# A perceiver layer with routed experts: matches, chunk constants and the first weight loads in other places of the last two tiles

## The reference

```python
x = x + xattn(layernorm(x), ctx, ...)      # 16 heads, each batch attends to its own 257 context rows of 192
x = x + local_attn(layernorm(x), ...)      # each row attends to rows i-2 .. i+2 of its batch
x = x + ffn(layernorm(x), ...)             # 8 experts, each token uses one: argmax(x @ Wr + br)
# ffn of expert e: gelu(x @ W1[e] + b1[e]) -> gelu(. @ W2[e] + b2[e]) -> . @ W3[e] + b3[e]
# sizes 256 -> 1024 -> 512 -> 256
```

## Time and profile before

| | |
|---|---|
| median of three runs | 708.14 us |
| the profiled execution | 709.04 us |
| its span, first to last instruction | 707.2 us |
| mean granted clock of TensorE | 0.992 |
| last scores of the tiles (batch 63) | start at 400.12 us |
| first row of experts enters TensorE | 428.59 us |
| busy: VectorE, ScalarE, GpSimd | 67%, 64%, 63% |

### The profile page before, as it was taken

The page is one execution under the profiler, slowest core; times in us unless marked ns, Lnnn a source line. Parts: engine busy times, 40 slices in busy tenths (PEclk is TensorE's granted clock), DMA queues, the critical chain, the costliest instruction groups (busy, mean ns, idle before and its releaser), DMA issues.

```text
span 707.2 us, 26666 instructions
## 1 busy us (share of the span) xinstructions
PE 687.9 (97%) x9301; PEld 581.3 (82%) x9302; DVE 475.2 (67%) x1462; ACT 451.4 (64%) x1073; POOL 442.9 (63%) x595
## 2 busy tenths in 40 slices
PE   8999999999999999999999969999999999999996
PEld 7888888888888888888888857888888888888885
DVE  4467777777777777777788889999943990278000
ACT  4656666666666676666666653666675757575753
POOL 6476665656566565656565635676767786777643
PEclk9999999999999999999999989999999999999998
DMA  7433233333323333343357324248034431262000
GB/s 214 119 87 85 70 78 96 93 82 82 96 72 93 94 88 74 76 96 91 87 154 246 129 83 165 97 123 300 23 106 159 170 113 60 82 223 65 25 7 1
DMA packets 56178, 74.35 MB, mean 105 GB/s; under 512 B 6589, under 2 KB 41950, under 8 KB 56128
## 3 DMA queue, kind: packets, MB, share of 16 engines
q1 hardware_dynamic: 49792, 60.63, 30.4%
q0 software_dynamic: 2992, 8.26, 3.8%
q10 hardware_dynamic: 3344, 4.80, 1.9%
HBM read 67.30 MB, written 7.27 MB: 105 GB/s over the span
## 4 chain that ended last, share of the span: by engine, by line
PE 92%; DVE 2%; issue 1%; ACT 1%; DMA 1%; POOL 1%; ACTq 0%; POOLq 0%; SPq 0%; DVEq 0%
PE ps_s L2023 18%; PE ps_kv L1603 12%; PE ps_kv L1611 11%; PE ps_p L1689 8%; PE ps_o L1675 6%; PE ps_s L1622 6%; PE ps_p L1971 4%; PE ps_kv L1971 4%; PE ps_o L2037 4%; PE ps_s L2002 2%; PE ps_m L1808 2%; PE ps_m L1754 2%; PE ps_m L1727 2%; PE ps_m L1812 2%; PE ps_s L2031 1%
## 5 line engine op out<-in xcount | busy, mean ns | idle before, releaser
L868 ACT ACTIVATE prob<-prob,neg_max 128x257 f32<-128x257 f32 x256 | 111.2, 501 | 42.9 <-DVE neg_max L1105 41.2
L1105 DVE CUSTOM_DVE_ANT_0 prob<-ps_s,mask_add 128x257 f32<-128x257 f32 x256 | 94.7, 421 | 64.0 <-PE ps_s L1622 63.7
L1573 DVE CAST w<-w_raw 128x512 fp32r<-128x512 f32 x94 | 71.0, 756 | 56.3 <-DMA w_raw<-in_L_ffn_W_dram 56.3
L1576 DVE TENSOR_TENSOR w<-w_raw,w 128x512 fp32r<-128x512 f32 x112 | 101.6, 910 | 3.7
L681 POOL TENSOR_TENSOR ctx_parts<-ctx_raw,ctx_parts 128x512 fp32r<-128x512 f32 x64 | 83.1, 1299 | 23.5 <-ACT ctx_parts L863 21.6
L2023 PE MATMUL ps_s<-w,h_hi 128*128 x368 | 91.1, 399 | 0.7 <-ACT h_hi L1017 0.6
L1611 PE MATMUL ps_kv<-wkv_hi,ctx_parts 128*128 128x256 f32 x512 | 84.6, 293 | 0.1
L1603 PE MATMUL ps_kv<-ctx_parts,wkv_hi 128*128 128x256 f32 x512 | 84.2, 292 | 0.2 <-POOL ctx_parts L681 0.2
L694 POOL COPY last_prob<-prob 128x4 f32<-128x4 f32 x64 | 12.1, 189 | 113.1 <-ACT prob L868 109.0
L876 ACT COPY v<-ps_kv 128x512 f32<-128x512 f32 x64 | 37.5, 587 | 70.2 <-PE ps_kv L1611 70.2
L806 POOL TENSOR_TENSOR h_lo<-h,h_hi 128x512 fp32r<-128x512 f32 x46 | 66.8, 1453 | 24.7 <-ACT h_hi L1004 19.8
(11 more groups left out here) (303 smaller groups left out, 1515.5 us busy)
## 6 DMA issues: line engine op xcount, KB each, us to landing
w_raw<-in_L_ffn_W_dram SPq DMA_DIRECT2D x24, 1024.0 KB, 7.1
ctx_raw<-in_ctx_turned_dram SPq DMA_DIRECT2D x63, 256.0 KB, 3.4
mask_add<-mask_dram SPq DMA_DIRECT2D x64, 128.5 KB, 3.3
w_raw<-in_L_ffn_W_dram SPq DMA_DIRECT2D x8, 512.0 KB, 3.6
rows_dram<-x3n ACTq DMA_DIRECT2D x15, 256.0 KB, 4.2
xt<-in_x_dram SPq DMA_DIRECT2D x16, 128.0 KB, 2.1
xr<-in_x_dram SPq DMA_DIRECT2D x16, 128.0 KB, 2.2
slot_x<-rows_dram,slot_ids POOLq DMA_INDIRECT x23, 3.9
```

The lines of the kernel that those rows point to most:

```text
L868: a.activation(prob[:, g, :], prob[:, g, :], ACT.Exp, bias=neg_max[:, g:g + 1], scale=-1.0).then_inc(exp_done, 1)
L1105: d.tensor_tensor_reduce(prob[:, r, :], ps_s[r][:, 0:J], mask_add[:, k, :], -(HD ** -0.5), 3.0e38, ALU.add, ALU.min, neg_max[:, r:r + 1]). ...
L1573: d.tensor_copy(w[:, b, HI, part], raw[:, b, part]).then_inc(rounded, 1)
L1576: last = d.tensor_tensor(w[:, b, LO, part], raw[:, b, part], f32(w[:, b, HI, part]), ALU.subtract)
```

## The change

Four edits.

1. Matches. VectorE takes eleven tiles and GpSimd five (tile 6 goes over). VectorE's matches of tiles 0 and 1 stand in (tile 15, k = 0) behind `number_many` and so ahead of the masks of that batch, that of tile 2 in (15, 1) ahead of the masks, those of tiles 3 and 4 at the two places in (15, 2). The match in (15, 3) and the one behind `number_single(1)` in `last_tile` are gone; the two later ones take tiles 5 and 6. GpSimd has no match in (15, 2); behind the tiles it makes four in a row (tiles 7 to 10), then the two scales, then the fifth (tile 11). TensorE's `fill_chunks` follow.
2. `place_chunks` goes from (1, 3) to (14, 3), behind `choose_single(0)` and ahead of the masks.
3. The eight `EARLY` loads are issued one after the other behind the load of the last residual rows (`xr` of tile 15), instead of one behind each mask load of tile 15, and one each behind four later events.
4. GpSimd issues the indirect load into `slot_x` (L780) ahead of `scale_of(2, 15)` and not behind it.

```diff
-        BY_DVE, BY_POOL = (0, 1, 2, 3, 12, 13, 4, 5, 14, 15), (6, 7, 8, 9, 10, 11)
+        BY_DVE, BY_POOL = (0, 1, 2, 3, 4, 12, 13, 5, 6, 14, 15), (7, 8, 9, 10, 11)
@@ SyncE
                     load_mask(T, b)
-                    if isinstance(T, int) and T == TILES - 1:
-                        load_part(*EARLY[b])
...
-            sp.wait_ge(m_emptied, turn(TILES - 2, 3) + 1)
-            load_x(xr, TILES - 2, xr_in)
-            load_part(*EARLY[BT])
-            sp.wait_ge(m_emptied, turn(TILES - 1, 3) + 1)
-            load_x(xr, TILES - 1, xr_in)
-            load_part(*EARLY[BT + 1])
-            sp.wait_ge(s_masked, GROUPS * B)
-            load_part(*EARLY[BT + 2])
-            sp.wait_ge(o_done, B)
-            load_part(*EARLY[BT + 3])
+            for T in (TILES - 2, TILES - 1):
+                sp.wait_ge(m_emptied, turn(T, 3) + 1)
+                load_x(xr, T, xr_in)
...
+            for part, e in EARLY:
+                load_part(part, e)
@@ GpSimd
-                    if isinstance(T, int) and (T, k) == (TILES - 1, 2):
-                        for t in BY_POOL[0:3]:
-                            match(t)
...
-            for t in BY_POOL[3:6]:
+            for t in BY_POOL[0:4]:
                 match(t)
             scale_of(1, TILES - 1)
             scale_of(2, TILES - 2)
+            match(BY_POOL[4])
...
-            scale_of(2, TILES - 1)
             g.indirect_dma_start(out=slot_x[:, AHEAD - 1, 0:D], ...)
+            scale_of(2, TILES - 1)
@@ VectorE
-                    if isinstance(T, int) and (T, k) == (1, 3):
-                        dve.wait_ge(router_consts, CONSTS)
-                        place_chunks()
...
                         choose_single(0)
+                        place_chunks()
                     if isinstance(T, int) and (T, k) == (TILES - 1, 0):
                         number_many()
+                        match(0)
+                        match(1)
+                    if isinstance(T, int) and (T, k) == (TILES - 1, 1):
+                        match(2)
                     if isinstance(T, int) and (T, k) == (TILES - 1, 2):
-                        match(0)
+                        match(3)
                     if isinstance(T, int) and (T, k) == (TILES - 1, 3):
                         number_single(0)
                         dve.wait_ge(logits_done, MANY + 2)
                         choose_single(1)
-                        match(2)
...
-                        match(1)
+                        match(4)
...
                 number_single(1)
-                match(3)
...
-                match(4)
+                match(5)
...
-                match(5)
+                match(6)
@@ TensorE
-                fill_chunks(0, 1, 2, 3, 6, 7, 8, 9)
+                fill_chunks(0, 1, 2, 3, 4, 7, 8, 9)
...
-                fill_chunks(10, 12, 11)
+                fill_chunks(10, 12)
...
-                fill_chunks(13, 4)
+                fill_chunks(13, 5)
...
-                fill_chunks(5)
+                fill_chunks(6, 11)
```

More of the change, by code:

```diff
@@ L535, in _ @@
             sp.dma_start(lbias[:, 4:6], lbv.rearrange("(c p) -> p c", p=P), allow_slow_non_contiguous=True).then_inc(router_in, 16)
[L537 to L547, removed]
             def ahead(T):
@@ L577, in _, with load_part @@
             ahead(TILES - 1)
-            sp.wait_ge(m_emptied, turn(TILES - 2, 3) + 1)
-            load_x(xr, TILES - 2, xr_in)
-            load_part(*EARLY[BT])
-            sp.wait_ge(m_emptied, turn(TILES - 1, 3) + 1)
-            load_x(xr, TILES - 1, xr_in)
-            load_part(*EARLY[BT + 1])
-            sp.wait_ge(s_masked, GROUPS * B)
-            load_part(*EARLY[BT + 2])
-            sp.wait_ge(o_done, B)
-            load_part(*EARLY[BT + 3])
+            for T in (TILES - 2, TILES - 1):
+                sp.wait_ge(m_emptied, turn(T, 3) + 1)
+                load_x(xr, T, xr_in)
+            def load_part(part, e):
+                _, raw, arrived, buffers, _ = PARTS[part]
+                b = turn_of(part, e) % buffers
+                if part == FIRST:
+                    w, n = W1[e], F1
+                elif part == THIRD:
+                    w, n = W3[e], D
+                else:
+                    half = HALVES.index(part)
+                    w, n = W2[e][half * F1 // 2:(half + 1) * F1 // 2, :], F2
+                sp.dma_start(raw[:, b, :].rearrange("p (k n) -> p k n", n=n), w.rearrange("(k p) n -> p k n", p=P)).then_inc(arrived[b], 16)
+            for part, e in EARLY:
+                load_part(part, e)
             sp.wait_ge(route, ROUTED)
@@ L705, in scale_of @@
                     g.tensor_tensor(spread[:, :], var_eps[i][:, :], rstd[i][:, :], ALU.mult).then_inc(spread_done, 1)
[L707 to L710, removed]
             def iteration(T):
@@ L767, in _, with match @@
             over_tiles(pool, iteration)
-            for t in BY_POOL[3:6]:
+            def match(t):
+                pool.wait_ge(many_step, 12)
+                g.tensor_scalar(of_chunk[:, t, :], chunk_number[:, :], chunk_at[:, t:t + 1], None, ALU.is_equal)
+                g.tensor_scalar(in_row[:, t, :], row_number[:, :], in_chunk[:, t:t + 1], tokens[:, t:t + 1], ALU.is_equal, ALU.mult).then_inc(matched_by_pool, 1)
+            for t in BY_POOL[0:4]:
                 match(t)
```

## The result

The changed kernel takes 713.1 us (711.92 to 714.16, six runs) against 708.69 us for the kernel before beside it (707.56 to 709.14): 1.0067 times as long, 95% interval 1.0056 to 1.0079. That is 4.4 us more; +1.5 was forecast, and the result lies above the range. The profiled execution took 714.08 us, its span is 712.3 us, and its mean granted clock 0.991; it is in the upper third of the 23 executions on record (711.92 to 714.81).

A forecast was written before the change was run, and what follows sets the result against it. TensorE was taken as the bound, except at batch 60, where VectorE's masks are. Terms +1.5 + 0.1 - 0.1 and zeros gave +1.5 us, 709.6 on the median of 708.14; eight-in-ten range 708.1 to 711.5.

The forecast's parts named there:

- The fall of the clock: Rival: between keys and values of batch 61 TensorE's longer gap halves the clock, +1.7 on top, 711.3 us; chance 0.18.
- Matches in (15, 0): Ahead of batch 60's masks: two matches, the first held up by GpSimd's shift, paid in full, +1.5 us.
- the rival without a hold-up: Rival at batch 60: GpSimd's shift does not hold `of_chunk`, the two matches cost 0.8, 708.9 us; chance 0.13.
- Match in (15, 1): Ahead of batch 61's masks: held up by GpSimd's shift, masks 0.7 late but mostly hidden, +0.1 us.
- the -0.1 of the sum: At (15, 3), one match less ahead of the masks of batch 63: -0.1 us, ends 0 and -0.5.
- `place_chunks` in (14, 3): Ahead of batch 59's masks: they start about 0.8 later, hidden by VectorE's idle time; cost 0, or 0.2 without cover.
- Where it leaves: In tile 1, where `place_chunks` is removed: the chain is TensorE's without a gap, gain 0.
- The loads: Eight loads behind `xr` of tile 15: hidden from ScalarE by 3 to 5 us of cover, 0, ends 0 and +0.5.
- the sign that I had named: The prediction is wrong if last scores to first expert row (28.5 us) changes by more than 0.3.
- Last tile's exchange of matches and the indirect load: In the last tile: VectorE's match gone, 0.1 gain, GpSimd's fourth match +0.1, indirect load in idle time 0; together 0.

The follow-up runs named there:

- only_matches_early: The kernel before, with the expert's number read by `value_load`, plus edits 1 and 4 (matches, indirect load) alone; 711.65 us, 1.0048 times the kernel before.
- the base: The kernel before with one edit, TensorE's slot loop reading the slot's expert by `value_load` into a plain register; 708.65 us, 1.0004 times the kernel before.
- loads_as_before: The changed kernel with the expert's number read by `value_load` and edit 3 undone, so loads spread as before; 713.16 us, 1.0070 times the kernel before.
- half pad: The kernel before, with `value_load`, `place_chunks` moved to tile 14 and two memsets put in (1, 3); 708.61 us, 1.0008 times the kernel before.

## Why the prediction was wrong

Two terms that stood in the sum with 0 failed: that `place_chunks` leaves its place ahead of the loop, which slowed the loop (+1.7 alone), and the burst of loads, which stopped TensorE (+0.8 alone). The fall of the clock stood outside the sum. What I had worked out from the rows, the hold-up in (15, 0), came as forecast.

**Matches in (15, 0): right in place, mechanism and size.** Forecast +1.5. From scores to masks it is 1.34 us more in the change and 1.46 in `only_matches_early`; `of_chunk` took 1.02, held by the shift, which is against the rival without a hold-up. Moved out of the shift's way they cost 0.2.

**Match in (15, 1): right, small.** Forecast +0.1, measured +0.15 to 0.2 from batch 60 to 63, held up by the shift until 392.1. The masks of batch 61 are 0.54 late (0.7 was forecast) and mostly covered. In (15, 3) the masks of batch 63 come 0.1 sooner after their scores, the -0.1 of the sum.

**`place_chunks` in (14, 3): right.** It hides: the masks of batch 59 come 0.76 later (0.8 was forecast), the scores of batch 60 only 0.13 later behind those of 59. **Where it leaves: wrong.** "In tile 1, where it leaves, the chain is TensorE's without a gap: gain 0." The 0 in the sum was the first failed step. I had bounded the edit by its own 0.8 us. What was removed is not only work but instructions ahead of a loop, and the loop ran 0.13 us a tile slower: +2.0 in the trace, +1.7 alone. The trace of before held a warning: that mask starts 1.08 us after the scores and the masks of the other batches 0.98, so at the jump VectorE and not TensorE was already the later one by 0.1.

**The loads: wrong.** "I take 0; ends 0 and +0.5." This is the second failed step. I asked who waits for the weights and for the rows beside them, and answered rightly that nobody does, though both came slower than I had counted: the first four loads landed 14.5 us after their first issue and not 9, and the store of rows at 400.73 took 6.9 us where 2.0 is usual. I did not ask what else uses those DMA engines. The instruction fetches do. In the trace 2.7 us of holes and the slower clock behind them make most of the +3.3 of the last tile, and the sign that I had named came: from the last scores to the first row it is 31.7 us and not 28.5. Alone the median is only +0.8; low executions are 1.9 to 2.7 above the base, the others 0.2 to 0.8. Both traces with the two holes are of low executions, so how large the holes are in the others is not shown.

**The clock: a rival that came beside the forecast.** I gave it 0.18 as something apart, at batch 61. It does happen there, in the trace of `loads_as_before`, and costs 1.2 us, not 1.7; the low executions of `only_matches_early` are 1.1 longer than the others, and where in them the clock fell no trace shows. In the profiled execution of the change it came at the second hole instead. Its weight should have been tied to the hold-up: the two kernels with the matches ahead of the masks and the early weights as before were low in seven of ten executions, against four of 97 of the kernel before.

**Last tile's exchange of matches and the indirect load: forecast 0, not told from 0.** 28.22 and 28.12 us from batch 63 to the first row with them, 27.77 without: +0.4, at the edge of the scatter of this stretch (27.20 to 28.21 in the kernels where it wasn't touched).

The parts alone are +1.7, +3.0 and +0.8, 5.5 in sum, against 4.4 to 4.5 together. The medians of the second and the third hold a fall of the clock in part of their executions, which can't count twice. Without the low executions the parts are +1.7, +1.9 and +0.4 against the base's 708.65, 4.0 in sum, and the changed kernel is at 712.81, 4.1 above the kernel before beside it. So the parts add up within the scatter, and the low executions lie 1.3 us above that.

## What to carry to other kernels

An edit ahead of a loop moves the loop: pad it, and measure the pass, before you blame what the edit does. Place work that is not urgent behind an engine's urgent instructions, above all where work of another engine would hold it up: the same matches cost 1.5 to 1.9 us ahead of the masks and 0.2 behind them. There is room for only so much: with `number_many` there as well, TensorE waited again. Where executions of one kernel come in two kinds, compare like with like before you say that an edit gained nothing. When loads are bunched, list all users of the DMA engines, fetches of instructions and later gathers too, and not only the readers of the data.

## What the runs showed that I had not expected

- With nothing changed in VectorE's loop, the first instruction behind its jump back came 1.19 or 1.07 us after the scores that it waits for, depending on how many instructions stand ahead of the loop; at the exit there was a hole of 0.46 (with four memsets), 0.30 (half pad) or none.
- TensorE stood still for 0.64 to 0.68 and 2.00 us in the middle of equal matmuls that wait for nothing, each time until 2.4 to 2.5 us after the start of a 16 KB fetch that came late beside a burst of loads at 376 to 411 GB/s.
- The Trainium skill (page "SBUF — State Buffer", section "Who interferes with whom") has VectorE's `tensor_scalar` in a two-port mode wait until the GpSimd instruction that was first has ended. The change's trace agrees, twice: 1.02 and 1.06 us beside a shift that had begun 0.1 and 0.2 before, 0.28 without.
